# Two projections of a cross-attention kernel turned round for two batches at a time

## The reference

```python
# layer 0: 32 query heads over 8 key heads, head size 16
q = x @ Wq + bq;  k = ctx @ Wk + bk;  v = ctx @ Wv + bv
s = einsum(q, k) * 16 ** -0.5 + mask
o = softmax(s) @ v
x1 = layernorm(o @ Wo + bo + x) * gamma + beta
# layer 1: one head of size 512
q1 = x1 @ w_q.T;  k1 = ctx @ w_k.T;  v1 = ctx @ w_v.T
out = x1 + alpha * (softmax(q1 @ k1.T * 512 ** -0.5) @ v1) @ w_o.T
```

## Time and profile before

| what | value |
|---|---|
| median of 3 runs (lowest to highest) | 756.72 us (755.82 to 762.5) |
| the profiled execution, its own time | 762.79 us |
| its span | 761.0 us |
| PE busy | 672.8 us, 88% of the span |
| DVE busy | 529.7 us, 70% |
| ACT busy | 390.1 us, 51% |
| POOL busy | 376.6 us, 49% |
| mean busy share of the 16 DMA engines, steady stretch | 0.63 to 0.68 |

### The profile page before, as it was taken

The page is one execution under the profiler, slowest core; times in us unless marked ns, Lnnn a source line. Parts: engine busy times, 40 slices in busy tenths (PEclk is TensorE's granted clock), DMA queues, the critical chain, the costliest instruction groups (busy, mean ns, idle before and its releaser), DMA issues.

```text
span 761.0 us, 13752 instructions
## 1 busy us (share of the span) xinstructions
PE 672.8 (88%) x3658; PEld 463.0 (61%) x3658; DVE 529.7 (70%) x1467; ACT 390.1 (51%) x589; POOL 376.6 (49%) x225
## 2 busy tenths in 40 slices
PE   5889788999999989899999999999989898988665
PEld 2546455767666657576766766666757676554433
DVE  1446676879696968868786879687877878774220
ACT  3222575565555555556555555556555565555101
POOL 5233566556465535565555646454546564445000
PEclk9999897999999999999999999999999999999989
DMA  8491857666656574757666665758584746523210
GB/s 308 192 148 58 134 144 172 155 163 133 164 157 152 172 148 145 162 131 176 160 164 158 133 172 150 156 160 152 173 155 138 178 121 150 111 84 113 85 52 11
DMA packets 60828, 110.15 MB, mean 145 GB/s; under 512 B 11662, under 2 KB 50126, under 8 KB 60027
## 3 DMA queue, kind: packets, MB, share of 16 engines
q1 hardware_dynamic: 60794, 109.76, 59.0%
HBM read 86.79 MB, written 22.52 MB: 144 GB/s over the span
## 4 chain that ended last, share of the span: by engine, by line
PE 39%; DMA 28%; SPq 16%; issue 10%; DVE 4%; POOL 1%; ACT 1%; POOLq 0%; DVEq 0%; ACTq 0%
DMA k_dr<-k_l 11%; DMA o_dr<-o_s 8%; PE work L606 6%; DMA qs<-mt_l 6%; PE work L593 5%; PE o_ps L525 4%; PE mx_ps L507 4%; SPq L289 4%; SPq L286 4%; SPq L302 3%; PE work L467 2%; PE work L468 2%; PE work L469 2%; PE sc_ps L492 2%; PE sc_ps L660 2%
## 5 line engine op out<-in xcount | busy, mean ns | idle before, releaser
L912 DVE CUSTOM_DVE_ANT_0 mx_ps<-mx_ps,mask_n 100x361 f32<-100x361 f32 x512 | 271.3, 545 | 109.4 <-PE mx_ps L507 100.8
L1412 POOL TENSOR_TENSOR pr<-pr,mask_t 128x800 f32<-128x800 f32 x128 | 256.5, 2011 | 157.6 <-ACT pr L1172 157.6
L507 PE MATMUL mx_ps<-ks,qs 96*100 96x362 f32 x512 | 186.4, 386 | 19.2 <-DMA qs<-q_dr 12.3
L1181 ACT ACTIVATE pr<-pr 128x1200 f32<-128x1200 f32 x128 | 152.3, 1203 | 21.7 <-DVE pr L896 17.6
L1172 ACT ACTIVATE pr<-sc_ps 128x800 f32<-128x800 f32 x128 | 106.8, 835 | 70.4 <-PE o_ps L525 44.8
L507 PEld LDWEIGHTS mx_ps<-ks,qs 96*100 96x100 f32 x512 | 86.2, 169 | 57.2 <-DVE mx L912 23.5
L1430 POOL TENSOR_TENSOR c_l<-cT,c_h 128x1448 fp32r<-128x1448 f32 x16 | 53.5, 3347 | 94.9 <-ACT c_h L1214 94.9
L896 DVE TENSOR_TENSOR pr<-sc_ps,mask_t 128x400 f32<-128x400 f32 x128 | 73.0, 570 | 9.5 <-PE sc_ps L488 9.5
L525 PE MATMUL o_ps<-pr,va 128*32 128x400 f32 (+1 forms) x768 | 72.9, 513 | 1.8 <-ACT pr L1181 1.8
L912 DVE DVE_READ_ACCUMULATOR2_ANT mx<- 100x1 f32 x512 | 72.2, 141 | 0.0
L492 PE MATMUL sc_ps<-qs,ks 98*128 98x400 f32 x128 | 55.8, 436 | 12.6 <-DMA qs<-mt_l 12.1
(11 more groups left out here) (121 smaller groups left out, 1193.2 us busy)
## 6 DMA issues: line engine op xcount, KB each, us to landing
qs<-q_dr SPq DMA_DIRECT2D x128, 100.0 KB, 4.3
late<-in_ctx SPq DMA_DIRECT2D x16, 768.0 KB, 5.0
cT<-in_ctxT SPq DMA_DIRECT2D x16, 724.0 KB, 5.8
ks<-k_dr SPq DMA_DIRECT2D x128, 90.5 KB, 4.1
late<-in_ctxT SPq DMA_DIRECT2D x16, 724.0 KB, 5.5
o_dr<-o_s SPq DMA_DIRECT2D x32, 200.0 KB, 3.1
xT<-in_xT SPq DMA_DIRECT2D x16, 200.0 KB, 3.4
q_dr<-q_h SPq DMA_DIRECT2D x16, 200.0 KB, 2.0
```

Of the source, the lines that this page charges most:

```text
L507: nc.tensor.matmul(mx_ps[0:L, n % 2, 0:SP2], qs[p][0:TERMS, g, L * j:L * (j + 1)], ks[p][0:TERMS, g, 0:SP2], start=True, stop=True).then_i ...
L912: V.tensor_tensor_reduce(out=src, in0=src, in1=mask_n[p][:, :], scale=1.0, scalar=-3.0e38, op0=ALU.add, op1=ALU.max, accum_out=mx[p][:, n: ...
L1181: A.activation(t, t, ACT.Exp).then_inc(ex_ok, 1)
L1412: G.tensor_tensor(t, t, mask_t[p][:, 1:3, :].unsqueeze(2).to_broadcast([P, 2, J, L]), ALU.add).then_inc(sc_pool, 1)
```

## The change

Both projections are made turned: a column block of the weights (128 columns) is the stationary operand and the activations move. Two batches go side by side in the moving operand, which then has 200 columns. The result comes out as the rest needs it, with the features on the partitions, so that the bias add in natural form, the copy of the natural result and both transposes are left out. Per pair and projection there are 4 column blocks by 4 row blocks by 3 instructions, 48.

- x_h, x_l, q_h, q_l, x1_h, x1_l are buffers for a pair of batches, xm_t is new. The query bias is a column, added by ACT and DVE while they split the result (two instructions of 200 columns on each engine where there was one of 400). The scale of 1/4 goes into Wq and the bias.
- `queries_out` writes a pair with two DMAs. q_dr and k_dr have a place for each of the 16 batches, so that writing them no longer waits for the reads of an earlier batch.
- To make room, vT takes the buffer of k_l (so `v_cols` waits until the keys of the batch are stored, and `k_low` until the values of the one before are turned), mt_h and mt_l are one buffer for both halves, den lies in `ones`, bv_b in xm_t, bo_r in y.
- One step handles two batches and its order is a new one on every engine; layer 1 of the odd batch falls a step later (offset -3). All steps are written out: the loop, its counters and `hold` are gone. There are 11 double steps, from -2 to 18.

```diff
-STEPS = (-2, B + 3)
+STEPS = (-2, B + 4)
-        xm_n = sb("xm_n", [L, H])
+        xm_t = sb("xm_t", [P, KT, 2, L])
-        vT = sb("vT", [P, SP2])
+        vT = k_l[:, :].bitcast(F32)
+                def q_part(off, o, h):
+                    b = i + off
+                    if o % 2 == 0 and h == 0:
+                        if o == 0:
+                            pe.wait_ge(xh_ok, b + 2)
+                            pe.wait_ge(xl_ok, b + 2)
+                        bank(1, f"q{o // 2}")
+                    cols, dst = slice(P * o, P * (o + 1)), work[:, 1, 2 * L * (o % 2):2 * L * (o % 2 + 1)]
+                    for k in range(2 * h, 2 * h + 2):
+                        mm = product(dst, wq_h[:, k, cols], wq_l[:, k, cols], x_h[:, k, :], x_l[:, k, :], k, KT - 1)
+                    if o % 2 == 1 and h == 1:
+                        mm.then_inc(q_mm, 1)
+                def xm_part(off, o, h):
+                            pe.wait_ge(x1h_ok, b + 2)
+                            pe.wait_ge(x1l_ok, b + 2)
+                        mm = product(dst, m_h[:, k, cols], m_l[:, k, cols],
+                                     x1_h[:, k, :, :].rearrange("p r l -> p (r l)"),
+                                     x1_l[:, k, :, :].rearrange("p r l -> p (r l)"), k, KT - 1)
-                def turn_q(off):
-                def turn_xm(off):
-                def q_natural(off):
-                def xm_row(off):
+                def q_low(off, o):
+                    src = work[:, 1, 2 * L * (o % 2):2 * L * (o % 2 + 1)].rearrange("p (r l) -> p r l", r=2)
+                    V.scalar_tensor_tensor(q_l[:, :, o, :], src, bq_c[:, o:o + 1], q_h[:, :, o, :].bitcast(F32),
+                                           ALU.add, ALU.subtract).then_inc(ql_ok, 1)
+                def v_cols(off):
                     act.wait_ge(v_mm, b + 1)
+                    act.wait_ge(k_out, 32 * (b + 1))
                     wait(act, v_tr, b)
```

More of the change, by code:

```diff
@@ L50, in emptied, with run_steps @@
         behind, before = divmod(at - back, len(users))
[L51 to L56, removed]
+        _, off, name, each, more, last = users[before]
+        batch = i + 2 * behind + off
+        if 0 <= batch <= last:
+            return name, each * batch + more
     return None, 0
 def wait(eng, sem, value):
-    if not (isinstance(value, int) and value <= 0):
+    if value > 0:
         eng.wait_ge(sem, value)
[L66 to L70, removed]
 def ring(b, par, dmas=1):
     return (8 * b - 8 * par + 16) * dmas
[L78 to L89, removed]
+def run_steps(body):
+    for i in range(STEPS[0], STEPS[1], 2):
+        body(i)
 def build(nc, xT_d, x_d, ctxT_d, ctx_d, mask_d, maskT_d, wq_d, wk_d, wv_d, wo_d, bq_d, bk_d, bv_d,
@@ L454, in _ @@
+                rows_in(0)
+                reciprocals_out(0)
+                mask_in(3)
+                stacks_in(2, 1, 2, 4)
+                rows_out(1, 0)
+                ctx_in(-2)
+                mask_turned_in(2)
+            run_steps(step)
             for p in range(2):
@@ new lines, in step @@
+                q_part(2, 2, 1)
+                heads(1, 16, 17)
+                q_part(2, 3, 0)
+                turn_maxima(1, 0)
+                scores(0, 6, 1, 3)
+                q_part(2, 3, 1)
+                scores(0, 5, 0, 1)
+                bias_row(-2)
+                heads(1, 17, 18)
+                y_part(-1, 0, 1)
+                scores(0, 7, 1, 3)
+                heads(1, 18, 19)
+                y_part(-1, 1, 2)
+                scores(0, 6, 0, 1)
+                k_part(2, 0, 1)
@@ new lines, in step @@
+                fold_n(-2, 2)
+                heads(2, 2, 3)
+                turn_v(2)
+                heads(2, 3, 4)
+                scores(1, 4, 0, 3)
+                heads(2, 4, 6)
+                values(1, 0)
+                heads(2, 6, 7)
+                k_part(3, 0, 1)
+                heads(2, 7, 8)
+                k_part(3, 1, 2)
+                turn_x1(-1)
+                heads(2, 8, 9)
+                scores(1, 5, 1, 3)
+                heads(2, 9, 10)
+                k_part(3, 2, 3)
@@ L836, in _ @@
+                y_part(0, 0, 1)
+            run_steps(step)
         @block.vector
@@ L1114, in step @@
[L1114 to L1117 removed]
+                maxima(3, 2, 4)
+                add_mask(2, 2)
+                maxima(3, 4, 5)
+            run_steps(step)
         @block.scalar
```

1003 lines of the change are left out of this document (565 added, 438 removed).

## The result

The changed kernel is slower: median 776.85 us (768.7 to 778.3, four runs) against 759.61 us (755.82 to 763.11, four runs) of the kernel before. The ratio is 1.0233, 95% interval 1.0179 to 1.0287. The forecast was 730, its range ended at 765. The profiled execution after took 776.33 us, its span is 774.3.

A forecast was written before the change was run, and what follows sets the result against it. PE was taken to set the 40.7 us period. Profiled 762.8 - 17 (projections) - 13 (waits) + 3 (ends) = 735.8, less 6.1 for the median: 730 us; own range 714 to 745, 8 in 10 708 to 765.

The forecast's parts named there:

- The ends: Start and tail of the run: loading, deferred late parts and earlier last attention together cost +3 us, between -3 and +12.
- The credit of 12 us: PE's late work, about 9 us a batch, leaves the full stretch, bringing the last attention forward by about 12 us.
- The late part at 13 us: Tail: the last two batches' late parts come one behind the other; one, s1 to residual, takes 13 us.
- Batch 13's part at "some 2 more": Tail: `d_part(-3)` of batch 13 adds some 2 us more to the serial late parts.
- the 17: Both projections on PE: 1.1 us saved a batch, 17 us over sixteen batches, between 12 and 23.
- the 13: PE's waits in the steady stretch: 1.0 of 2.5 us a batch gained over 13 batches, 13 us, ends 0 and 32.
- The projections' price: Turned projections on PE: 24 instructions a batch at 107 ns, 2.57 us for 3.12, saving 0.55 us each.
- The narrow stream: Rival, 768 new projection instructions: 200 columns cost more (median 787 or 928), or weight loads don't overlap (794). Chance 0.14.
- Waits for `v_cols` or the keys' store: Rival: ACT held by the keys' store, 3 to 5 us a pair, idles PE and eats all gains; 757 us. Chance 0.10.
- The loop: Writing out the steps: counted inside the waits' gain, with no term of its own.
- PE's content falls and nothing else: Rival: the new order on PE has as many waits, so only the 17 us are saved; 745 us. Chance 0.15.
- the chance of 0.17: Total chance of a slower kernel, carried by dearer 200-column instructions and a tail of the waits.

The follow-up runs named there:

- eight-batch kernels: The kernel before, written out, and the changed kernel, each run over only the first eight batches: 438.07 and 468.47 us, one run each.
- Idle products: Changed kernel with unread products on PE ahead of its waits in the last steps: median 764.97 us; the same in the kernel before: 763.05 us.
- four and two terms: Changed kernel with one more or one fewer instruction per product of the two turned projections: 788.44 and 755.48 us, single runs.
- the kernel with the new order: Changed kernel with batch 13's late part moved ahead of batch 15's output projection in the last double step: median 775.58 us, ratio 1.019 to the kernel before.
- order and idle products together: Changed kernel with batch 13's late part ahead of the last output projection and unread products ahead of PE's waits: median 758.97 us, ratio 0.9962 to the kernel before.

## Why the prediction was wrong

**The step that failed is "The ends"**, "Net +3 us, between -3 and +12". Measured: +43.7 in the profiled execution, +6.3 at the start and +37.4 in the tail. It was made of 13 + 2 - 12:

- *The credit of 12 us*, for PE's late work "leaving the full stretch ahead of it for one or two batches", was not paid. The work did leave, but from the filling (PE 31.59 us busy for 37.95), and the 9th `values` came 6.3 us later, not 12 earlier. PE waits there for DVE's maxima, 8.2 us in the window of the filling. 4.6 of it are one wait, behind one instruction of the layer norm: `centre` took 5.75 us on DVE while POOL multiplied the mask in. The wait of PE, the two engines' timelines, and the same instruction in all batches of the kernel before (shortest, median and longest in ns):

```profile
PE mx_ps L513 <- DVE mx L992: 8.2, 3, 4.6
...
189.15 5.75 DVE L1117 TENSOR_SCALAR y<-y,mv,rstd 100x512 f32<-100x512 f32 x1
...
189.06 5.55 POOL L1565 TENSOR_TENSOR pr<-pr,mask_t 128x800 f32<-128x800 f32 x3
...
L1042 DVE TENSOR_SCALAR y<-y,mv,rstd x16: 545/547/549, 142.1 to 733.4; 100x512 f32<-100x512 f32 x16
```

  The other 3.6 us of the wait stand behind `centre` and `gain` of batch 0, which were stretched too (3.49 and 2.37 us for 0.55 and 0.69), and from 168.2 to 176, right after them, PE's clock is 0.56. That these make the 6.3 us is read from the trace; no run tests it. That the loss at the start is fixed is shown by the eight-batch kernels (+6.0).
- *The late part at 13 us.* The row that it was read from ran at the upper clock, 1.00. In the new tail the same part runs at 0.71 and costs 17.8 us, twice. The windows of batch 14's part, before and after:

```profile
714.40:727.60 13.20, 9.65 (x43) 5.54 (x43) 2.63 (x6) 2.06 (x6) 0.00 (x0) 1.00 0.38 125
...
735.59:753.39 17.80, 14.26 (x43) 8.07 (x43) 1.66 (x4) 1.64 (x5) 0.00 (x0) 0.71 0.26 86
```

  Idle products give 16.7 us of the tail back and 12 us of the median. Nothing in the prediction asked what the clock would do where two serial chains follow one another without other work.
- *Batch 13's part at "some 2 more".* Its `residual` and the 2.94 us store from x stand ahead of `gain` of batch 15: 17.6 us from `y_sum` to `gain` (704.63 to 722.27), where the kernel before has 3.2. The buffer's next user was not looked up. Part of it is the low clock again, but with idle products the same two are still 13.0 us apart (708.33 to 721.30); the order that moves it measured nothing by itself and, with the clock held, brought the median from 764.97 to 758.97.

Against the forecast's +3 this is 12 + 6.3 at the front and 22.4 more in the tail than the 15 it had (13 + 2): 40.7 us in all. Of the 22.4, 12.7 are the clock (16.7 less the 4.0 that idle products take off the kernel before) and 9.7 the longer chain. With the 40.7 the forecast of 730 becomes 770; the median was 777. The last 6 us are the 6.1 that the forecast took off because the profiled execution lay that far above the median. That median came from three runs. With the fourth the distance is 3.2, and in the later sets of 17 to 29 runs the kernel before has medians of 760.7 to 762.8, close to the profiled 762.79; after's profiled run (776.33) is at its median too.

**The steady period was right; that the sum fits to 0.3 us is in part luck, and its division was off.** Forecast was a period of 38.6 us a batch, measured 307.3 / 8 = 38.4. Forecast 17 + 13 = 30 us; measured 30.3 in the profiled pair. But the 17 was for sixteen batches and the 13 for thirteen, and the middle has 11.5: at the forecast's 2.1 us a batch that makes 24. It measured 2.1 to 2.6 a batch over all pairs, and a few us may be late work that left the middle for the tail, so a part of the credit of 12: the middle gains 11.7 us in 3.5 batches and 30.3 in 11.5, which is 2.3 a batch and 3.6 beside it. The projections' price was right: 0.112 us a product for 0.107 forecast, so 24 x 0.112 = 2.69 us, 0.43 saved a projection, 0.86 a batch. But four and two terms put what reaches the period at 0.55 to 0.7 of that, 0.4 to 0.9 with their spread: 0.3 to 0.8 us a batch, 5 to 12 us for the 17. The rest of the 2.3 to 2.6 us, 1.5 to 2.3 a batch where the forecast had 1.0, came with the new order or the other parts of the change; no run takes these apart, and the slopes are of single profiles. PE's waits in the kernel after, 298.4 to 605.7, agree in kind with it:

```profile
PE mx_ps L513 <- DVE mx L992: 7.1, 11, 1.2
PE sc_ps L494 <- DMA qs<-mt_l: 1.0, 2, 0.6
PE sc_ps L498 <- DMA qs<-mt_l: 0.9, 1, 0.9
```

The wait of `turn_x1` for the layer norm, the largest of the earlier trace rows, is gone as forecast, and the one for the maxima's DMAs is down from 4.5 us in six batches to 1.9 in eight; a new one, heads for DVE's maxima, stands in their place. Together they are 9.0 us in 8 batches, 1.1 a batch for 2.5 before.

**The rivals.** The narrow stream is refuted, in both forms: the limit was 130 ns, the row has 112. Waits for `v_cols` or the keys' store appear nowhere. The loop, put at nothing, is nothing. The rival that PE's content falls and nothing else is out as well: 1.1 us a batch for 2.5. The sign came out on the slower side, but by none of the mechanisms that carried the chance of 0.17; a loss at the ends beyond +12 had no chance of its own. The missing rival was the ends themselves, with a point that can be worked out: they decide once they cost more than the 30 us that the middle gives.

## What to carry to other kernels

Deferring work by a step costs at the ends, once, and the steady stretch can't show it: count separately what the filling loses, what the tail gains in serial chains, and what a batch saves, and see how many batches it takes to pay (here 20 to 22, and there are 16). Cut both traces at a marker instruction into start, middle and tail before reading anything else. Price a drain made of latencies at both clock levels (13.2 or 17.8 us for the same part here), and count a buffer that serves an earlier batch there as part of the chain. When a new order moves instructions of one engine beside those of another, check whether single instructions have grown: here 0.55 us became 5.75.

## What the hardware showed that was not expected

- Products that nobody reads, put into PE's pauses, made the kernel 12 us faster (776.85 to 764.97): the tail went from 96.2 to 79.5 us and its clock from 0.77 to 0.98.
- At the lower level, the distance of the 200-column products is 0.21 us (chain at 726.47), in the full stretch 0.11. `d_part` is 3.65 us in one and 6.6 in the other.
- Three instructions of the layer norm on DVE grew several times over when an instruction of POOL had begun before them. In the kernel before, `shift` took 2.26 to 2.42 us in 14 of 16 batches and 0.69 in the other two. In the changed kernel `centre` took 2.12 to 5.75 us in eleven batches (0.55 otherwise) and `gain` 2.37 to 3.61 in three (0.69 otherwise). In each of these 28 cases an instruction of POOL had begun before and was still running; where one began only behind the start of the DVE instruction (11 cases), that kept its 0.69.
- The last `values` follows the one before by 20.3 us in the kernel with the new order, by 15.8 in the changed kernel, though the new order begins behind it. In between, `shift` took 2.24 us for 0.69, again beside POOL, PE stood idle for 3.7 us and not 1.4, and the clock of the stretch is 0.83 and not 1.00. With order and idle products together it also fell, to 0.82, behind only 1.7 us; so why it falls stays open. The tail also differs between kernels whose order there is the same: 96.2 us at a clock of 0.77 in the changed kernel, 84.5 at 0.92 with four terms, 87.8 at 0.82 with two.
